# Short f32 side products counted as half a unit of fill in a recurrence, and one transposition a step later

## The chip, the cores and the metric

The kernel runs on one core of one Trainium2 chip. The metric is the device time of one execution in microseconds (us), lower is better. The kernel before takes 1494.18 us in the median of three runs (1492.56 to 1495.71).

## The reference

The input x has four batches of 256 rows of 512. Four layers are added to it one after the other, each on a layer norm of x: a cross-attention, a gated feed-forward with int4 weights (1792 wide), a recurrent attention decoder over the 256 rows, and a feed-forward with 16 experts of which two are taken for each row. The decoder is the part that matters here, since each of its 256 steps needs the one before:

```python
def step(carry, tgt):
    s, c, alpha = carry
    f = lax.conv_general_dilated(alpha, conv_w, (1,), 'SAME', dimension_numbers=('NCH', 'OIH', 'NCH'))
    e = jnp.einsum('a,bta->bt', va, jnp.tanh(enc_proj + (s @ Wa_s.T)[:, None, :] + jnp.einsum('bft,af->bta', f, Wa_f) + ba))
    e = jnp.where(mask, e, jnp.float32(-1e+30))
    alpha_new = jax.nn.softmax(e, axis=1)[:, None, :]
    g = jnp.einsum('bt,btd->bd', alpha_new[:, 0], hbatch)
    y = jnp.tanh(g @ L_gy_w.T + L_gy_b + s @ L_sy.T) @ L_yy_w.T + L_yy_b
    rec = tgt @ L_ys.T + s @ L_ss.T + g @ L_gs_w.T + L_gs_b
    ig, fg, cg, og = jnp.split(rec, 4, axis=1)
    c_next = _sig(fg) * c + _sig(ig) * jnp.tanh(cg)
    s_next = _sig(og) * jnp.tanh(c_next)
    return ((s_next, c_next, alpha_new), y)
```

The targets tgt are rows of the layer norm of x after the second layer. Row l of the fourth layer needs y of step l.

## The kernel before, in words

A front part computes the attention of all rows and the first feed-forward of the first quarter of the rows. Then the recurrence runs its 256 steps (`for l in range(S)`, once in each engine's program). An end part does the experts of the last quarter.

One step of the recurrence is a chain over three engines. TensorE adds the state's part (L1876, L1882), ScalarE takes a tanh twice, in f16 and in f32 (L1438, L1439), TensorE makes the scores (L1890, L1896, and L1899 once VectorE's low part of the tanh is ready), ScalarE takes the exponentials (L1443, L1444), TensorE multiplies with them (L1908, L1913) and with VectorE's low part el (L1917 and on), VectorE normalises, ScalarE and VectorE make the gates and the new state, and TensorE's L1933 carries the attention into the next step.

TensorE would wait at five places of a step. There it calls `fill(units, order, rest)`, at L1886, L1897, L1901, L1930 and L1934, called fill 1 to 5 below, for 1, 1, 2, 2 and 1.5 units: 7.5 units a step, counted in half units (`HALF_UNIT, UNIT = 1, 2`). A fill adds its units to `credit` and takes work from generators until the credit is used up; what each piece of work yields is what it costs. If nothing is due, it issues a product without use, `keep_busy` (L1854), of 512 columns for a unit (384 in fill 1).

The work comes from two generators. `main_work` has the two feed-forwards for the other quarters: f16 products of 256 columns for half a unit (L1647, L1685, the experts' weights L1701) and of 512 for a unit (L1664). `side_work` has short f32 products that get layer norms, the decoder's inputs and outputs and the experts' routing through TensorE:

- `turn`: transpositions of 128x128 blocks of a layer norm (L1723), four for each half of a quarter's rows;
- `gates_input`: after a turn, the f32 products for the gates (L1560, not changed), two for a unit;
- `prelude`: outputs of the decoder (L1760, L1762), then rows products (L1805, 65x128, each two instructions on TensorE), then a turn;
- `expert_routing`: router products (L1769, 16 columns, each two instructions), two for a unit, then two transpositions of the expert weights (L1777).

Fills 1 and 2 ask main work first, fills 3 to 5 side work first. Each generator is held back by `paced(step)`: it gives nothing before the step that a table sets (`LN2`, `GATES`, `Y`, `PRELUDE`, `first_step`). A main tile of 24 products is spread over two steps, 12 half units a step. In a step with two transpositions of a unit each, side and main work want 4 + 12 = 16 half units of 15, and main work falls behind its table by a product or two. The order in which TensorE issues is fixed by this when the program is built; the waits on semaphores stay in it, so an instruction whose wait is late holds all that stand behind it.

In `gates_input` the last turn (q = 3, p = 1, table entry 165, so step 172) also waits for `rin_ready`, which ScalarE raises after its second gate piece of the half before (L1360).

Of the kernel before, what the change touches and what calls it, by code (L numbers as in the profile page):

```python
# [81 lines left out]
def build(nc, a, out):  # L82
    with ExitStack() as ctx:
# [280 lines left out]
        def pace(q):  # L364

            return 4 if q == 2 else 2

        def prelude_step(q, name, p=None):

            if q == 3:  # L370
                return S
            n = PRELUDE[q][name]
            return Y[q] + (n if p is None else n[p])
# [10 lines left out]
        def gates_bank(q, p):  # L384
            return bank[5 if q == 3 else 5 + p]
# [13 lines left out]
        def ln3(q, p):  # L399
            return (12, 16, 22, 26)[q] + p  # L400

        def ln4(q, p):
            return (20, 24, 28, 30)[q] + p
# [14 lines left out]
        def paced(step):  # L418

            while now[0] < step:  # L420
                yield False
# [1060 lines left out]
        def _(pe):  # L1482
# [73 lines left out]
            def gates(slot, bk, signal):  # L1556

                for gp in range(2):
                    for kt in range(KT):
                        last = mm(bk[:, gp * P:(gp + 1) * P], lys[:, kt, gp * P:(gp + 1) * P], xT_rec[:, kt, :], start=(kt == 0), stop=(kt == KT - 1))  # L1560
                        if signal and gp == 1 and kt == KT - 1:
                            last.then_inc(s["rec_done"], 1)
                        yield True
# [68 lines left out]
            HALF_UNIT, UNIT = 1, 2  # L1632
# [83 lines left out]
            def turn(n, bk, t, per_step):  # L1716

                for kt in range(KT):
                    yield from paced(t + kt // per_step)
                    if kt == 0:  # L1720
                        pe.wait_ge(s["ln_ready"], n + 1)
                        pe.wait_ge(s["xT_ready"], n - 1)
                    last = nc.tensor.transpose(bk[:, kt * P:(kt + 1) * P], xn[:, n % 2, kt * P:(kt + 1) * P], ident[:])  # L1723
                    if kt == KT - 1:
                        last.then_inc(s["tr_done"], 1)
                    yield UNIT

            def next_input(q):
                for p in range(2):
# [5 lines left out]
            def gates_input(q):  # L1735
                for p in range(2):
                    t, slot, bk = GATES[q][p], 2 * q + p, gates_bank(q, p)
                    yield from paced(t + 7)
                    if q == 1:
                        pe.wait_ge(s["xl_ready"], 5 + p)  # L1740
                    elif q == 2:
                        pe.wait_ge(s["wT_low_ready"], 1)
                    else:
                        pe.wait_ge(s["xT_ready"], ln4(1, 1) + 1)
                    if q == 3 and p == 1:
                        pe.wait_ge(s["rin_ready"], slot)
                    yield from turn(ln3(q, p), bk, t + 7, 2)
                    work = gates(slot, bk, True)
                    for unit in range(8):
                        yield from paced(t + 11 + p + unit // 2)  # L1750
                        if unit == 0:
                            pe.wait_ge(s["xT_ready"], ln3(q, p) + 1)
                        next(work)
                        yield UNIT

            def outputs(q):

                bk, rows = y_bank(q), slice(q * QL, (q + 1) * QL)
                for h in range(2):
                    mm(bk[0:J, 0:QC], hy[:, h, :], ahist[:, rows, 4 * h:4 * h + 4], start=(h == 0), stop=False)  # L1760
                    yield UNIT
                mm(bk[0:J, 0:QC], lsyT[:], shist[:, rows, :], start=False, stop=True).then_inc(s["y_done"], 1)  # L1762
                yield UNIT
# [18 lines left out]
            def prelude(q):  # L1782
                work = outputs(q)
                for unit in range(3):
                    yield from paced(prelude_step(q, 'outputs') + 2 * unit // pace(q))
                    if unit == 0:
                        pe.wait_ge(s["hist_done"], (q + 1) * QL)
                        pe.wait_ge(s["kept"], (q + 1) * QL)
                        if q == 0:
                            pe.wait_ge(s["xl_ready"], 8)  # L1790
                        elif q == 1:
                            pe.wait_ge(s["rin_ready"], 6)
                        else:
                            pe.wait_ge(s["wT_low_ready"], 2)
                    next(work)
                    yield 2 * UNIT
                for p in range(2):
                    for part in range(4):
                        yield from paced(prelude_step(q, 'rows', p) + part // pace(q))
                        if part == 0:  # L1800
                            pe.wait_ge(s["u_ready"], q + 1)
                            pe.wait_ge(s["w1_in"], 32)
                            if q == 2 and p == 1:
                                pe.wait_ge(s["y_added"], 2 * q + 1)
                        last = mm(rows_bank(q, p)[:, P * part:P * part + P], uT[:, q % 2, p * P:(p + 1) * P], lyy[:, P * part:P * part + P],  # L1805
                                  start=True, stop=True)
                        if part == 3:
                            last.then_inc(s["yy_done"], 1)
                        yield UNIT
                for p in range(2):  # L1810
                    yield from paced(prelude_step(q, 'turn', p))
                    pe.wait_ge(s["y_added"], 2 * q + 2)
                    if q == 2:
                        pe.wait_ge(s["act_ready"], TILES + 2 * IT1)
                    yield from turn(ln4(q, p), turn_bank(q, p), prelude_step(q, 'turn', p), pace(q))

            def expert_routing(q):
                work = router(q)
                for unit in range(8):
                    yield from paced(prelude_step(q, 'router') + unit // 4)  # L1820
                    if unit == 0:
                        pe.wait_ge(s["xT_ready"], ln4(q, 1) + 1)
                        if q == 1:
                            pe.wait_ge(s["rin_ready"], 8)
                    next(work)
                    if unit % 2 == 1:
                        yield UNIT
                work = turn_weights(q)
                for unit in range(2):
                    yield from paced(prelude_step(q, 'turned'))  # L1830
                    if unit == 0:
                        pe.wait_ge(s["wsel_ready"], q + 1)
                    next(work)
                    yield UNIT

            def side_work():
                yield from next_input(2)
# [190 lines left out]
```

## Time and profile before

| | |
|---|---|
| median of 3 runs | 1494.18 us (1492.56 to 1495.71) |
| the profiled execution, its own time | 1494.22 us |
| its span | 1492.3 us |
| mean granted clock of TensorE | 0.936 |
| TensorE busy | 1372.9 us, 92% of the span |
| VectorE, ScalarE, GpSimd busy | 892.8, 585.8, 210.0 us |
| chain of waits that ended last: TensorE, VectorE, ScalarE | 83%, 7%, 5% |
| filler products (L1854) | 685, 194.7 us busy |

The recurrence runs from about 287 to 1440 us of the span. Busy times overlap between engines. Matmuls are pipelined: each lasts some 0.16 us longer than the time until the next can start, so in a row of several equal ones the time goes by their spacing. The granted clock is the share of full speed that the chip gave to TensorE in a stretch; 1.00 is 2.4 GHz and 0.50 is 1.2 GHz, and what lies between is a mean of the two.

### The profile page before, as it was taken

To read this page: it belongs to the slowest core of one execution; us is meant where nothing else is said; L and a number is where in the kernel's file an instruction comes from. 1 tells how busy PE (TensorE), PEld (TensorE's weight loads), DVE (VectorE), ACT (ScalarE), POOL (GpSimd) and SP (SyncE) were. 2 spreads that over 40 slices of the span, in tenths; PEclk is the share of its full clock that TensorE was granted. 3 is DMA by queue.
4 is the path that set the end of the run, shared out by engine and by line. 5 is a ranking of instruction groups with operands and counts; after the bars stand their busy time and mean duration, and the time that the engine had idled before them with its cause. 6 is when DMAs were issued, how large, how long until landed. Compare 5 with 4: busy or idle time off the path is not lost.

```text
span 1492.3 us, 41237 instructions
## 1 busy us (share of the span) xinstructions
PE 1372.9 (92%) x16128; PEld 864.9 (58%) x16128; DVE 892.8 (60%) x4447; ACT 585.8 (39%) x2367; POOL 210.0 (14%) x704
## 2 busy tenths in 40 slices
PE   3466887999999999999999999999999999999988
PEld 1345665566655666655566655556655665566546
DVE  3664754366655566575666657766655566566643
ACT  3553652234333344333334434443433333333321
POOL 1001002011111121111111112231110011111111
PEclk8666897999999999899999999999999999999999
DMA  8462220000000000000000001110000000000000
GB/s 280 190 219 77 78 77 4 1 2 2 2 2 2 2 2 2 2 2 2 2 2 2 2 19 51 55 36 2 2 16 2 2 2 9 9 2 2 9 9 15
DMA packets 23863, 44.77 MB, mean 30 GB/s; under 512 B 8788, under 2 KB 12035, under 8 KB 23668
## 3 DMA queue, kind: packets, MB, share of 16 engines
q1 hardware_dynamic: 23668, 42.14, 8.5%
q8 instruction: 126, 2.06, 0.6%
q14 instruction: 69, 0.57, 0.1%
HBM read 40.04 MB, written 2.10 MB: 28 GB/s over the span
## 4 chain that ended last, share of the span: by engine, by line
PE 83%; DVE 7%; ACT 5%; issue 4%; SPq 1%; DMA 1%; POOL 0%; DVEq 0%; ACTq 0%; POOLq 0%
PE bank L1933 10%; PE bank L1854 10%; PE bank L1647 9%; PE bank L1876 8%; PE bank L1664 6%; PE bank L1908 6%; PE bank L1685 4%; PE bank L1890 3%; PE bank L1624 3%; PE bank L1917 3%; PE bank L1896 2%; PE bank L1882 2%; PE bank L1630 2%; PE bank L1532 2%; ACT interT L1210 2%
## 5 line engine op out<-in xcount | busy, mean ns | idle before, releaser
L1854 PE MATMUL bank<-ctx_lgs,identh 128*128 128x512 f16 (+2 forms) x685 | 194.7, 358 | 0.0
L1933 PE MATMUL bank<-ker_mem,uh 128*128 128x128 f32 x1020 | 185.9, 306 | 1.0 <-DVE ker_mem L1133 0.8
L1933 PEld LDWEIGHTS bank<-ker_mem,uh 128*128 128x128 f32 x1020 | 138.3, 196 | 71.2 <-DVE ker_mem L1133 70.5
L1647 PE MATMUL bank<-xT,wbig 128*128 128x256 f16 x1008 | 168.9, 280 | 0.0
L1452 ACT ACTIVATE xs<-gat 64x8 f32<-64x8 f32 x255 | 52.9, 207 | 245.5 <-DVE gat L1129 245.4
L1438 ACT ACTIVATE ker_mem<-bank 128x128 f16<-128x128 f32 x256 | 71.0, 277 | 187.0 <-PE bank L1876 187.0
L1443 ACT ACTIVATE eh<-bank,nmx 128x8 f16<-128x8 f32 x256 | 68.4, 267 | 160.8 <-PE bank L1899 160.8
L1664 PE MATMUL bank<-wbig,interT 128*128 128x512 f16 x378 | 124.8, 393 | 0.0
L1133 DVE TENSOR_TENSOR ker_mem<-inv,ahn 128x128 f32<-128x128 f32 x510 | 124.0, 285 | 0.1
L709 POOL TENSOR_TENSOR sscale<-ex,rinv 128x8 f32<-128x8 f32 x256 | 51.1, 200 | 496.4 <-DVE rinv L1118 496.4
L705 POOL COPY sscale<-s 64x4 f32<-64x4 f32 x256 | 59.2, 231 | 388.4 <-DVE s L1148 388.4
L1908 PEld LDWEIGHTS bank<-eh,ctx_lgs 128*128 128x128 f16 x2048 | 69.5, 96 | 69.4 <-ACT eh L1443 68.9
L1115 DVE TENSOR_TENSOR el<-ex,eh 128x8 f16<-128x8 f32 x256 | 43.0, 168 | 105.9 <-ACT ex L1444 105.8
L1107 DVE TENSOR_TENSOR ker_mem<-enc,ker_mem 128x128 f16<-128x128 f32 x256 | 74.8, 292 | 45.2 <-ACT enc L1439 44.1
L1118 DVE RECIPROCAL rinv<-bank 128x4 f32<-128x4 f32 x256 | 46.7, 182 | 78.8 <-PE bank L1917 78.8
L1455 ACT ACTIVATE tc_sb<-xs 64x4 f32<-64x4 f32 x255 | 52.4, 205 | 105.6 <-DVE xs L1144 105.6
L1908 PE MATMUL bank<-eh,ctx_lgs 128*128 128x4 f16 x2048 | 90.2, 166 | 1.9
L1532 PE MATMUL bank<-vbd,interT 128*128 128x34 f32 x256 | 47.2, 343 | 45.2 <-ACT interT L1218 45.2
L1876 PEld LDWEIGHTS bank<-sh,was 64*128 64x128 f16 x512 | 28.4, 94 | 102.8 <-DVE sh L1147 97.1
L1104 DVE TENSOR_TENSOR rs<-bank,rin 128x8 f32<-128x8 f32 x256 | 42.1, 164 | 73.9 <-PE bank L1882 62.4
L591 POOL TENSOR_TENSOR interT<-work,interT 128x256 f16<-128x256 f32 x84 | 56.6, 674 | 187.4 <-ACT interT L1229 115.1
L1876 PE MATMUL bank<-sh,was 64*128 64x128 f16 x512 | 73.7, 225 | 8.4 <-DVE sh L1147 0.6
(232 smaller groups left out, 3130.3 us busy)
## 6 DMA issues: line engine op xcount, KB each, us to landing
kbd<-d_keys SPq DMA_DIRECT2D x32, 256.0 KB, 3.7
wbig<-d_gate_qT SPq DMA_DIRECT2D x4, 896.0 KB, 9.9
wbig<-d_up_qT SPq DMA_DIRECT2D x4, 896.0 KB, 20.6
wbig<-d_down_qT SPq DMA_DIRECT2D x1, 3584.0 KB, 13.1
sscale<-d_down_sT SPq DMA_DIRECT2D x4, 768.0 KB, 8.8
x_sb<-d_x SPq DMA_DIRECT2D x16, 128.0 KB, 2.9
d_out<-x_sb SPq DMA_DIRECT2D x16, 128.0 KB, 2.4
sscale<-d_gate_sT SPq DMA_DIRECT2D x2, 896.0 KB, 8.3
```

The lines of the kernel that those rows point to most:

```text
L1107: nc.vector.tensor_tensor(th_lo, th, th_hi, ALU.subtract).then_inc(s["th_lo_ready"], 1)
L1133: return nc.vector.tensor_tensor(qv[:, h, :, :], inv[:].unsqueeze(1).broadcast_to([P, B, TH]), ahn[:, 4 * h:4 * h + 4].unsqueeze(2).broadc ...
L1438: nc.scalar.activation(th_hi, bank[0][:, 0:P], ACT.Tanh).then_inc(s["th_s"], 1)
L1443: nc.scalar.activation(eh[:], bank[0][:, P:P + 8], ACT.Exp, bias=nmx[:, 0:1]).then_inc(s["eh_ready"], 1)
L1532: last = mm(bank[6 + pair // 8][:, (pair % 8) * 34:(pair % 8) * 34 + 34], pT[:, n % 2, j * P:(j + 1) * P], vbd[:, b, pair // 2, :], start= ...
L1647: last = mm(tile_bank(n)[:, lo:lo + QC], w[wi][:, kt, it * P:(it + 1) * P], x_part[q % 2][xi][:, kt, :], start=(kt == 0 and wi + xi == 0), ...
L1664: last = mm(bk[:], i_part[ii][:, it, p * P:(p + 1) * P], w[wi][:, it, :], start=(it == 0 and ii + wi == 0), stop=(it == tiles - 1 and ii = ...
L1685: last = mm(tile_bank(n)[:, lo:lo + QC], w[wi][:, kt, it * P:(it + 1) * P], x1_part[q][xi][:, kt, :], start=(kt == 0 and wi + xi == 0), st ...
L1854: mm(bank[7][:, 0:n], identh[:], hg2[:, 0].rearrange("p h g -> p (h g)")[:, 0:n], start=True, stop=True)
L1876: last = mm(bank[0][:, 0:P], was2[:, j, :], st[:].unsqueeze(2).broadcast_to([J, B, TH]), start=False, stop=(st is sl), skip_group_check=True)
L1908: mm(bank[2][:, 8 + 4 * gp:12 + 4 * gp], hg2[:, j, h, gp * P:(gp + 1) * P], e[:, 4 * h:4 * h + 4], start=False, stop=final, skip_group_che ...
L1933: mm(bank[0][:, 0:P], uh[:, h, :], qv[:, h, :, :], start=False, stop=False, skip_group_check=True)
```

## The change

Transpositions, rows products, pairs of router products and transpositions of expert weights yield `HALF_UNIT` instead of `UNIT`. The last turn of the gate inputs begins one step later, in step 173. The other costs, the tables and the sizes of the fills stay.

```diff
@@ turn
                     last = nc.tensor.transpose(bk[:, kt * P:(kt + 1) * P], xn[:, n % 2, kt * P:(kt + 1) * P], ident[:])
                     if kt == KT - 1:
                         last.then_inc(s["tr_done"], 1)
-                    yield UNIT
+                    yield HALF_UNIT
@@ gates_input
                     t, slot, bk = GATES[q][p], 2 * q + p, gates_bank(q, p)
-                    yield from paced(t + 7)
+                    yield from paced(t + 7 + (q == 3 and p == 1))
...
-                    yield from turn(ln3(q, p), bk, t + 7, 2)
+                    yield from turn(ln3(q, p), bk, t + 7 + (q == 3 and p == 1), 2)
@@ prelude
                         if part == 3:
                             last.then_inc(s["yy_done"], 1)
-                        yield UNIT
+                        yield HALF_UNIT
@@ expert_routing
                     next(work)
                     if unit % 2 == 1:
-                        yield UNIT
+                        yield HALF_UNIT
                 work = turn_weights(q)
...
                     next(work)
-                    yield UNIT
+                    yield HALF_UNIT
```

Only TensorE's order changes, in 74 of the 256 steps. Three places of it follow. L1647, L1685 and L1664 are main products, L1854 filler, L1890 to L1917 and L1933 the recurrence's own.

Step 9, fill 3, which follows L1899, with two transpositions; before:

```order
L1899 MATMUL bank<-vae,ker_mem 128x8
L1723 MATMUL bank<-ident,xn 128x128 x2
L1908 MATMUL bank<-eh,ctx_lgs 128x4 x8
L1913 MATMUL bank<-eh,onesb 128x4 x2
L1917 MATMUL bank<-el,onesb 128x4 x2
```

and with the change:

```order
L1899 MATMUL bank<-vae,ker_mem 128x8
L1723 MATMUL bank<-ident,xn 128x128 x2
L1647 MATMUL bank<-xT,wbig 128x256 x2
L1908 MATMUL bank<-eh,ctx_lgs 128x4 x8
L1913 MATMUL bank<-eh,onesb 128x4 x2
L1917 MATMUL bank<-el,onesb 128x4 x2
```

Two main products of 256 columns stand beside the transpositions; fill 5 of the step ends with a filler of 256 columns in place of the third main product. In steps with rows products it is the same with L1805.

Step 183, fills 1 to 3, with router products; before:

```order
L1769 MATMUL bank<-gwT,kbd 128x16 x2
L1890 MATMUL bank<-ker_mem,vah 32x32 x8
L1896 MATMUL bank<-vae,ker_mem 128x8 x2
L1769 MATMUL bank<-gwT,kbd 128x16 x2
L1899 MATMUL bank<-vae,ker_mem 128x8
L1854 MATMUL bank<-ctx_lgs,identh 128x512 x2
L1908 MATMUL bank<-eh,ctx_lgs 128x4 x8
```

and with the change:

```order
L1769 MATMUL bank<-gwT,kbd 128x16 x4
L1890 MATMUL bank<-ker_mem,vah 32x32 x8
L1896 MATMUL bank<-vae,ker_mem 128x8 x2
L1854 MATMUL bank<-ctx_lgs,identh 128x512
L1899 MATMUL bank<-vae,ker_mem 128x8
L1854 MATMUL bank<-ctx_lgs,identh 128x512 x2
L1908 MATMUL bank<-eh,ctx_lgs 128x4 x8
```

All four router products of the step stand in fill 1, and fill 2 has a filler of 512 columns.

Step 172, from its fill 2 on, where the moved turn began; before:

```order
L1685 MATMUL bank<-interT,wbig 128x256 x2
L1899 MATMUL bank<-vae,ker_mem 128x8
L1723 MATMUL bank<-ident,xn 128x128 x2
L1908 MATMUL bank<-eh,ctx_lgs 128x4 x8
L1913 MATMUL bank<-eh,onesb 128x4 x2
L1917 MATMUL bank<-el,onesb 128x4 x2
```

and with the change the turn begins in fill 1 of step 173:

```order
L1701 MATMUL bank<-interT,wbig 128x256
L1723 MATMUL bank<-ident,xn 128x128
L1890 MATMUL bank<-ker_mem,vah 32x32 x8
L1896 MATMUL bank<-vae,ker_mem 128x8 x2
L1723 MATMUL bank<-ident,xn 128x128
L1854 MATMUL bank<-ctx_lgs,identh 128x256
L1899 MATMUL bank<-vae,ker_mem 128x8
```

Its last two transpositions stand in fill 3 of step 174, beside a main product of 512 columns.

## Rows read from the trace of the kernel before

**Rows 1.** Stretches: bounds, us, busy by engine (instructions), granted clock, DMA; plain steps
```profile
382.84:471.51 88.67, 88.07 (x1158) 51.96 (x1155) 53.23 (x316) 33.01 (x152) 11.63 (x46) 1.00 0.01 2
690.13:694.57 4.44, 4.30 (x58) 2.31 (x55) 3.06 (x17) 1.98 (x8) 1.05 (x3) 1.00 0.00 0
```

**Rows 2.** Timeline of TensorE in step 5, a plain one: start, us, instruction
```profile
311.13 0.38 PE L1647 MATMUL bank<-xT,wbig 128*128 128x256 f16 x2
311.39 0.18 PE L1899 MATMUL bank<-vae,ker_mem 128*128 128x8 f16 x1
311.42 0.60 PE L1647 MATMUL bank<-xT,wbig 128*128 128x256 f16 x4
311.93 0.35 PE L1908 MATMUL bank<-eh,ctx_lgs 128*128 128x4 f16 x8
...
312.29 0.20 PE L1917 MATMUL bank<-el,onesb 128*128 128x4 f16 x2
```

**Rows 3.** Stretches with f32 side products, or just behind them
```profile
337.31:347.12 9.81, 9.66 (x124) 6.52 (x120) 5.90 (x33) 4.04 (x18) 1.43 (x5) 0.83 0.01 2
610.38:636.81 26.43, 26.32 (x309) 18.49 (x306) 15.05 (x83) 8.61 (x39) 3.90 (x13) 0.74 0.01 2
667.99:685.71 17.72, 17.23 (x222) 9.83 (x219) 9.66 (x61) 6.93 (x30) 1.51 (x8) 1.00 0.01 2
884.18:901.91 17.73, 17.47 (x230) 11.13 (x226) 11.08 (x64) 7.17 (x30) 2.32 (x8) 1.00 0.06 15
699.27:709.29 10.02, 10.00 (x119) 6.21 (x116) 5.19 (x32) 3.10 (x15) 1.42 (x5) 0.83 0.01 2
811.79:821.90 10.11, 9.79 (x126) 6.48 (x123) 5.58 (x32) 4.61 (x19) 1.43 (x5) 0.83 0.01 2
1062.78:1074.09 11.31, 10.28 (x120) 6.73 (x116) 5.96 (x34) 4.03 (x17) 1.42 (x5) 0.70 0.01 2
1119.06:1124.85 5.79, 5.79 (x65) 3.96 (x61) 2.50 (x15) 1.49 (x7) 0.38 (x2) 0.72 0.01 3
1282.06:1293.07 11.01, 11.01 (x120) 7.07 (x116) 5.30 (x33) 3.10 (x16) 2.10 (x6) 0.69 0.11 25
```

**Rows 4.** Stretches: router steps 90 and 183, at full clock
```profile
694.57:699.27 4.70, 4.70 (x65) 3.11 (x62) 2.42 (x16) 1.49 (x7) 1.05 (x3) 1.00 0.01 3
1114.22:1119.06 4.84, 4.81 (x65) 3.19 (x62) 2.51 (x16) 1.50 (x8) 0.38 (x2) 1.00 0.24 56
```

**Rows 5.** Timeline of TensorE in step 9, with two transpositions in fill 3
```profile
329.19 0.18 PE L1899 MATMUL bank<-vae,ker_mem 128*128 128x8 f16 x1
329.28 0.41 PE L1723 MATMUL bank<-ident,xn 128*128 128x128 f32 x2
329.73 0.35 PE L1908 MATMUL bank<-eh,ctx_lgs 128*128 128x4 f16 x8
```

**Rows 6.** Timeline of TensorE in step 90, router products in fill 3
```profile
695.40 0.18 PE L1899 MATMUL bank<-vae,ker_mem 128*128 128x8 f16 x1
...
696.33 0.34 PE L1908 MATMUL bank<-eh,ctx_lgs 128*128 128x4 f16 x8
...
696.58 0.19 PE L1917 MATMUL bank<-el,onesb 128*128 128x4 f16 x2
```

**Rows 7.** Timeline of TensorE in step 132, two rows products in fill 3
```profile
885.01 0.18 PE L1899 MATMUL bank<-vae,ker_mem 128*128 128x8 f16 x1
...
885.62 0.34 PE L1908 MATMUL bank<-eh,ctx_lgs 128*128 128x4 f16 x8
```

**Rows 8.** Timeline of step 172: TensorE and, first, ScalarE; idle before in brackets
```profile
1064.14 0.58 ACT L1360 ACTIVATE rin<-bank,gbias,gscale 128x128 f32<-128x128 f32 x1
...
1063.61 0.18 PE L1899 MATMUL bank<-vae,ker_mem 128*128 128x8 f16 x1
1064.82 0.41 PE L1723 MATMUL bank<-ident,xn 128*128 128x128 f32 x2 [1.03 <-ACT rin L1360]
...
1065.32 0.19 PE L1917 MATMUL bank<-el,onesb 128*128 128x4 f16 x2
```

## The prediction, before the change was run

> **What bounds the kernel now.** I read the page first, then the stretches of the recurrence, then single steps on TensorE. Steps are numbered 0 to 255, and step l begins where ScalarE starts its first tanh (L1438). The recurrence is most of the program, and nearly every step takes the same time: twenty plain steps take 88.67 us at a granted clock of 1.00, 4.43 us each [rows 1]. That length is the chain through TensorE, ScalarE and VectorE, not the amount streamed: the step at 690.13, step 89, whose five fills hold 14 half units instead of 15, takes 4.44 us too [rows 1]. So work in a fill is free as long as it ends before its wait does. How tight that is shows in a plain step: from the start of L1899 to the start of L1908, which waits for the exponentials, 0.54 us pass (311.39 to 311.93), with four 256-column products between; the sum products (L1917) start 0.36 us later, at 312.29, and wait for VectorE's el [rows 2].
>
> The second thing the page shows is a clock that is not always granted in full. I cut the recurrence into stretches at step starts: those much longer than 4.43 us per step are the ones with a granted clock under 1.00 [rows 3]: the engine ran part of them at 1.2 GHz instead of 2.4. Every one that I found but that of step 0 lies in steps that hold short f32 side products (transpositions, rows, router) or just after them. TensorE did not idle there: in 610.38 to 636.81 it was busy for 26.32 of 26.43 us, and still the clock was 0.74. What it did before the clock fell was f32 side work in the place of wide f16 products. The Trainium skill, "TensorE: Matmul & The Clock Gate", section "Part 4: PE-mode transpose", says that a transposition does not count as busy in the same way as a product; the trace agrees for the transposition steps 11 and 63, but the clock also fell in steps with rows and router products, which are no transpositions.
>
> **Low clock, priced.** From each stretch I take 4.434 us per step [rows 3]. Steps 11 and 12: 9.81 - 8.87 = 0.94; steps 63 and 64 are a second pair with the same length and clock, 0.94. Steps 72 to 76 (rows products): 26.43 - 22.17 = 4.26. Steps 116 and 117: 10.11 - 8.87 = 1.24. Steps 172 and 173: 11.31 - 8.87 = 2.44, of which 0.8 is a stall (below), so 1.64. These are the steps of transpositions and rows: 9.0 us. The router's: steps 91 and 92, 10.02 - 8.87 = 1.15; step 184, 5.79 - 4.43 = 1.36; steps 220 and 221, 11.01 - 8.87 = 2.14. The router products themselves cost 0.27 in one step and 0.41 in each of two at full clock (steps 90 and 183 [rows 4]), which leaves 0.88 + 0.95 + 1.73 = 3.6 us for the clock.
>
> **The change, part by part.** It alters what TensorE issues in 74 steps; the order on the other engines stays. No product is added to the computation: 64 transpositions, 24 rows products, 12 pairs of router products and 6 transpositions of weights count one half unit less, 106 in all, and the fills make that up with 33 filler products (L1854) of 512 columns, 39 of 256 and one of 192, since the main products get done sooner.
>
> *Transpositions.* In 24 steps a fill that held two transpositions or more now gets something beside them or more of them. Before, two transpositions take 0.41 us and L1908 starts 0.54 us after L1899, as in a plain step, although TensorE is done much earlier [rows 5]. Four 256-column products take 0.60, two of them 0.38 [rows 2], so two more cost 0.22; 0.41 + 0.22 = 0.63, against the 0.60 that the plain step hides. L1917 has 0.36 us after L1908 in the plain step and needs 0.25 (step 90 [rows 6]), so 0.11 of cover is left. Cost: nothing. If that cover is gone, some 0.1 us in each of 24 steps, 2.4 us.
>
> *Rows products (L1805).* Two of them (four instructions) bring L1908 to 0.61 us after L1899 [rows 7]; this is 0.07 late and hidden by the 0.11. With 512 columns more it is 0.61 + 0.22 + 0.25 = 1.08 us to L1917 instead of 0.90: 0.18 in each of seven steps (72, 73, 75, 132 to 135), 1.26. In steps 200 and 206 four of them now share fill 3. Eight router instructions fill the 0.93 us from L1899 to L1908 in step 90, 0.116 each [rows 6], and four more rows instructions are taken at that: 0.61 + 4 x 0.116 + 0.25 - 0.90 = 0.4 a step, 0.8 for both. Step 74 has its two rows products in fill 1, about 0.14.
>
> *Router products (L1769).* In steps 90 and 91 they already overfill fill 3: L1917 comes 0.25 + 0.93 = 1.18 us after L1899, 0.28 over plain, and the step is 4.70 [rows 6, 4]. Nothing hides a further 0.22: 0.43 for both. In steps 183, 184, 219 and 220 the second half of them moves from fill 2 to fill 1 and 512 columns of filler take their place: 0.22 each, 0.86.
>
> Overfull steps together: 1.26 + 0.8 + 0.14 + 0.43 + 0.86 = 3.5 us. The trace has no step with just these mixes; the bounds are nothing beyond what now stands (0, if the waits have slack that I don't see) and 3.5 + 2.4 = 5.9. I take 3.5, since the router rows show such a delay arriving in the step length almost whole.
>
> *The transposition a step later.* In step 172 the four transpositions of the last gate input begin with a wait for ScalarE's L1360, the second gate piece: it starts at 1064.14, runs 0.58, and L1723 starts at 1064.82 after 1.03 us of idle [rows 8]. L1908, L1917 and so the whole step queue behind it: L1917 comes 1.71 us after L1899 (1063.61 to 1065.32) against 0.90 in a plain step, 0.8 us. They now begin in step 173, long after L1360. ScalarE takes the result in the late half of step 174, and the last transposition is issued in fill 3 of 174, before it; on VectorE nothing moves. So 0.8 goes and no new wait comes.
>
> *The clock.* In a transposition or rows step the fill now streams 512 columns beside the f32 work, 0.22 us more of wide f16 products, which brings it back to what plain steps have, less at most the f32 work's own share. No plain step fell. My forecast is that the 9.0 us go and the router's 3.6 stay, since there the streamed share stays low for a whole step.
>
> **Sum.** 1494.22 (the profiled execution, span 1492.3; the median of the runs is 1494.18, so nothing has to be moved) - 9.0 - 0.8 + 3.5 = 1487.9 us. Its own range is 1486 to 1490.
>
> **Rivals.**
> *Router stretches go too.* The 512 columns in steps 90, 183, 219 and their like may be enough. Then 3.6 more go: 1484.3. Against it: two router steps in a row still hold sixteen f32 instructions with 16 columns each. Chance 0.08.
>
> *Some falls only move.* Steps 84 to 87 hold transpositions and kept the clock at 1.00, so did the rows steps 132 to 135 (17.73 us for four, 4.43 each), whereas steps 11 and 72 to 76 didn't [rows 3]: it is partly chance which group falls. If the longer, overfull steps 72 to 75, 132 to 135, 200 and 206 fall in their place, half of the 9.0 comes back: 1487.9 + 4.5 = 1492.4. Chance 0.2.
>
> *Slower: the filling does not hold the clock.* If it falls for some other reason than a lack of wide f16 products, the 12.6 us of low clock stay and only the price is new: 1494.2 - 0.8 + 3.5 = 1496.9. It decides from the point where the clock saves under 2.7 us, in the steps 72 to 76. For it speaks that TensorE was busy all the time where the clock fell. The Trainium skill, "TensorE: Matmul & The Clock Gate", section "HAM oscillation", puts a falling clock down to idle gaps between groups of products; by that rule more filling would change nothing here, and the result would be this one. The rows don't bear it out: step 172 has the longest gap and the clock fell there, but in 72 to 76 there is none [rows 3, 8]. Chance 0.1.
>
> *The change doesn't do what it says.* The same number of columns could pile up on TensorE as the bound: 33 x 512 + 39 x 256 + 192 = 27072 columns at 0.22 us per 512 are 11.6 us. The step at 690.13 excludes it for most: fewer columns there bought nothing [rows 1]. Chance 0.02, at 1505.
>
> **Chances.** The forecast has 0.6. A measurement of this kernel can tell about 0.2%, 3 us, from no change; faster by more means under 1491.2. Forecast and the first rival are there nearly whole, the second with a third of its chance: 0.75. Within 0.2%: the rest of the second and a little of the first, 0.16. Slower: 0.09 with the last two rivals and a price above 3.5. The range takes in the forecast and most of the second rival and leaves out the router's gain and the slower cases: 1485.2 to 1492.8.
>
> **What would show it.** Right: clock 1.00 in steps 9 to 12, 62 to 65, 72 to 76 and 116; a mean granted clock well over 0.936 in the recurrence; L1723 with no idle before it in step 173 and step 172 at 4.43; steps 132 to 135 at 4.6, 200 and 206 at 4.8, 90 at 4.9 and 183 at 5.05. Wrong: transposition steps over 4.5 at full clock, which says that 0.11 of cover isn't there; or stretches at half clock in the same number as before, elsewhere.

## The result, and the profile after

The changed kernel takes 1483.77 us in the median of five runs (1482.95 to 1484.96) against 1494.18 for the kernel before (1491.19 to 1495.71): a ratio of 0.9928, interval 0.9901 to 0.9955. The forecast was 1487.9 with a range of 1485.2 to 1492.8. The sign is right; the time lies 1.4 us under the range. Its profiled execution took 1483.51 us with a span of 1481.6, against 1494.22 and 1492.3; the mean granted clock rose from 0.936 to 0.947.

Stretches of the changed kernel, cut at step starts as in [rows 1, 3, 4] (bounds, us, busy by engine, granted clock, DMA). First the recurrence, whole, then twenty plain steps, 9 to 12, 72 alone, 72 to 76, 90, 91 and 92, 116 and 117, 132 to 135, 172, 173 and 174, 183, 184, 200, and 220 with 221:

```profile
283.45:1429.42 1145.97, 1135.82 (x14934) 697.17 (x14930) 722.64 (x4160) 449.77 (x1983) 173.46 (x618) 0.99 0.03 8
378.15:466.79 88.64, 88.00 (x1158) 51.93 (x1154) 53.24 (x316) 33.00 (x151) 11.62 (x46) 1.00 0.01 2
324.62:342.43 17.81, 17.67 (x252) 12.07 (x249) 12.01 (x67) 7.61 (x34) 2.86 (x10) 1.00 0.01 2
604.73:609.35 4.62, 4.59 (x68) 3.33 (x65) 2.46 (x16) 1.77 (x9) 1.05 (x3) 1.00 0.01 4
604.73:627.70 22.97, 22.83 (x315) 15.54 (x312) 14.76 (x83) 8.61 (x40) 3.89 (x13) 1.00 0.01 3
685.45:690.37 4.92, 4.90 (x66) 3.21 (x62) 2.41 (x16) 1.49 (x7) 1.04 (x3) 1.00 0.00 0
690.37:699.72 9.35, 9.29 (x121) 5.61 (x118) 5.10 (x32) 3.10 (x15) 1.42 (x5) 1.00 0.01 2
802.23:811.09 8.86, 8.80 (x128) 5.92 (x124) 5.49 (x32) 4.61 (x19) 1.43 (x5) 1.00 0.01 2
873.36:891.72 18.36, 18.28 (x236) 11.45 (x233) 11.05 (x64) 7.16 (x30) 2.30 (x8) 1.00 0.05 14
1052.53:1056.96 4.43, 4.40 (x65) 2.84 (x61) 3.08 (x18) 1.96 (x9) 1.05 (x3) 1.00 0.02 6
1056.96:1066.98 10.02, 10.00 (x117) 5.91 (x113) 6.01 (x34) 3.82 (x18) 1.43 (x5) 0.83 0.01 2
1102.69:1107.74 5.05, 5.02 (x66) 3.27 (x62) 2.51 (x16) 1.49 (x7) 0.38 (x2) 1.00 0.23 54
1107.74:1113.54 5.80, 5.80 (x66) 3.92 (x63) 2.50 (x15) 1.49 (x7) 0.38 (x2) 0.78 0.01 3
1180.74:1185.58 4.84, 4.82 (x70) 3.59 (x67) 3.09 (x18) 1.49 (x8) 1.05 (x3) 1.00 0.00 0
1271.92:1282.35 10.43, 10.40 (x121) 6.50 (x117) 5.24 (x33) 3.10 (x15) 2.10 (x6) 0.84 0.11 27
```

Each row gives the bounds, the length, the busy time of TensorE, its weight loads, VectorE, ScalarE and GpSimd with their instructions, the granted clock and the DMA share and rate. A plain step is as long as before. The clock is now 1.00 in steps 11, 12, 72 to 76, 91, 92, 116 and 117, where it was low in [rows 3]. It still falls in 173, 184 and 220, as it did before. The overfull steps show their price at full clock: 4.62 in step 72, 4.92 in step 90, 5.05 in step 183, 4.84 in step 200. Step 172 is plain again.

Why step 72 is 0.18 us longer and step 9 isn't stands in TensorE's timeline. Step 9 of the changed kernel:

```profile
325.45 0.18 PE L1899 MATMUL bank<-vae,ker_mem 128*128 128x8 f16 x1
325.55 0.41 PE L1723 MATMUL bank<-ident,xn 128*128 128x128 f32 x2
325.79 0.38 PE L1647 MATMUL bank<-xT,wbig 128*128 128x256 f16 x2
326.01 0.34 PE L1908 MATMUL bank<-eh,ctx_lgs 128*128 128x4 f16 x8
326.43 0.20 PE L1917 MATMUL bank<-el,onesb 128*128 128x4 f16 x2
```

L1908 starts 0.56 us after L1899 and L1917 0.98 us after it. In the kernel before L1917 was as late in this step (329.19 to 330.17), so the two products more are hidden. Step 72 of the changed kernel:

```profile
605.56 0.18 PE L1899 MATMUL bank<-vae,ker_mem 128*128 128x8 f16 x1
605.66 0.68 PE L1805 MATMUL bank<-interT,sscale 65*128 65x128 f32 x4
606.18 0.38 PE L1647 MATMUL bank<-xT,wbig 128*128 128x256 f16 x2
606.40 0.34 PE L1908 MATMUL bank<-eh,ctx_lgs 128*128 128x4 f16 x8
```

L1908 starts 0.84 us after L1899 instead of 0.61 [rows 7], which is 0.3 late against the plain step's 0.54. In step 200, with eight rows instructions in the fill, it is 1.06 (1181.57 to 1182.63):

```profile
1181.57 0.18 PE L1899 MATMUL bank<-vae,ker_mem 128*128 128x8 f16 x1
1181.67 1.13 PE L1805 MATMUL bank<-interT,sscale 65*128 65x128 f32 x8
1182.63 0.34 PE L1908 MATMUL bank<-eh,ctx_lgs 128*128 128x4 f16 x8
```

**Where the 10.7 us between the two spans went.** The recurrence is 1145.97 us long against 1153.00 (from 287.18 to 1440.18 before): 7.0 less. The end part is 52.2 us in both. The other 3.7 lie ahead of the first step, where no instruction differs. The next rows are everything ahead of the first tanh of step 0, the dense part of it, and the recurrence, of the kernel before:

```profile
0.00:287.18 287.18, 190.88 (x991) 137.14 (x991) 152.00 (x232) 126.75 (x360) 27.14 (x70) 0.77 0.35 120
206.80:244.40 37.60, 32.58 (x190) 26.90 (x191) 13.62 (x25) 15.81 (x50) 3.36 (x5) 0.73 0.04 8
287.18:1440.18 1153.00, 1139.62 (x14861) 699.39 (x14858) 723.07 (x4160) 449.85 (x1983) 173.63 (x618) 0.98 0.03 8
```

and of the changed kernel:

```profile
0.00:283.45 283.45, 190.34 (x991) 137.24 (x991) 151.93 (x232) 126.89 (x360) 27.16 (x70) 0.77 0.36 122
206.80:244.40 37.60, 31.30 (x207) 26.06 (x207) 16.50 (x32) 16.41 (x52) 4.10 (x6) 0.82 0.04 7
```

The mean clock of the front part is the same, but in the dense stretch from 206.80 to 244.40 it is 0.82 instead of 0.73, and TensorE gets through 207 products there instead of 190. Whether this is chance or belongs to the changed kernel is what the second and third profiles below are for.

### The profile page after: what moved, and what is told of

Its sections match the earlier page's. It is cut to its first block, busy times and chain, and to the rows that moved or that the text cites. A ratio compares the mean times of both kernels' runs of the same rounds, so it can differ in the third digit from the quotient of the medians.

```text
span 1481.6 us, 41383 instructions
## 1 busy us (share of the span) xinstructions
PE 1368.7 (92%) x16201; PEld 862.8 (58%) x16201; DVE 892.4 (60%) x4447; ACT 585.8 (40%) x2367; POOL 209.8 (14%) x704
## 4 chain that ended last, share of the span: by engine, by line
PE 84%; DVE 6%; ACT 4%; issue 3%; SPq 1%; DMA 1%; POOL 0%; DVEq 0%; ACTq 0%; POOLq 0%
PE bank L1854 10%; PE bank L1933 10%; PE bank L1647 9%; PE bank L1876 8%; PE bank L1664 7%; PE bank L1908 6%; PE bank L1685 4%; PE bank L1890 3%; PE bank L1624 3%; PE bank L1917 3%; PE bank L1896 2%; PE bank L1882 2%; PE bank L1630 2%; PE bank L1532 2%; ACT interT L1210 2%
## 5 line engine op out<-in xcount | busy, mean ns | idle before, releaser
L1854 PE MATMUL bank<-ctx_lgs,identh 128*128 128x512 f16 (+2 forms) x758 | 211.2, 352 | 0.0
L1933 PE MATMUL bank<-ker_mem,uh 128*128 128x128 f32 x1020 | 182.8, 302 | 0.6 <-DVE ker_mem L1133 0.6
L1933 PEld LDWEIGHTS bank<-ker_mem,uh 128*128 128x128 f32 x1020 | 134.7, 192 | 71.2 <-DVE ker_mem L1133 71.0
L1647 PE MATMUL bank<-xT,wbig 128*128 128x256 f16 x1008 | 165.3, 274 | 0.0
L1664 PE MATMUL bank<-wbig,interT 128*128 128x512 f16 x378 | 125.6, 391 | 0.0
L1908 PEld LDWEIGHTS bank<-eh,ctx_lgs 128*128 128x128 f16 x2048 | 69.4, 96 | 67.1 <-ACT eh L1443 64.4
L1908 PE MATMUL bank<-eh,ctx_lgs 128*128 128x4 f16 x2048 | 90.0, 166 | 0.3
L1876 PEld LDWEIGHTS bank<-sh,was 64*128 64x128 f16 x512 | 28.3, 94 | 101.8 <-DVE sh L1147 99.3
L1147 DVE SCALAR_TENSOR_TENSOR sh<-xs,tc_sb 64x4 f16<-64x4 f32 x255 | 39.3, 154 | 69.3 <-ACT tc_sb L1455 69.3
```

The source lines that it names most:

```text
L1647: last = mm(tile_bank(n)[:, lo:lo + QC], w[wi][:, kt, it * P:(it + 1) * P], x_part[q % 2][xi][:, kt, :], start=(kt == 0 and wi + xi == 0), ...
L1664: last = mm(bk[:], i_part[ii][:, it, p * P:(p + 1) * P], w[wi][:, it, :], start=(it == 0 and ii + wi == 0), stop=(it == tiles - 1 and ii = ...
L1854: mm(bank[7][:, 0:n], identh[:], hg2[:, 0].rearrange("p h g -> p (h g)")[:, 0:n], start=True, stop=True)
L1876: last = mm(bank[0][:, 0:P], was2[:, j, :], st[:].unsqueeze(2).broadcast_to([J, B, TH]), start=False, stop=(st is sl), skip_group_check=True)
L1908: mm(bank[2][:, 8 + 4 * gp:12 + 4 * gp], hg2[:, j, h, gp * P:(gp + 1) * P], e[:, 4 * h:4 * h + 4], start=False, stop=final, skip_group_che ...
L1933: mm(bank[0][:, 0:P], uh[:, h, :], qv[:, h, :, :], start=False, stop=False, skip_group_check=True)
```

## The experiments

All are edits of the kernel before or of the changed kernel, in four groups, each on another chip; the kernels of a group ran beside the kernel before in the same rounds, so times are compared within a group. In the expectations a "stretch of low clock" is the shortest fall that was seen, and a longer fall counts as several. To compare, I give the recurrence's length and the clock of its critical steps in each profile. Counted over the recurrence, the profiles have these stretches of low clock:

| kernel | stretches | recurrence, us |
|---|---|---|
| before: first profile, e1, e13 | 14, 32, 24 | 1153.0, 1170.1, 1163.5 |
| the move alone: e2 | 19 | 1156.8 |
| 16 columns beside: e9, e16 | 12, 15 | 1153.4, 1157.5 |
| 256 columns beside: e4, e15 | 7, 9 | 1150.0, 1153.5 |
| halved costs alone: e3, e14 | 10, 7 | 1152.9, 1149.7 |
| changed: first profile, e5, e12 | 4, 4, 8 | 1146.0, 1146.2, 1150.3 |
| transpositions alone: e7; fuller: e8 | 7; 7 | 1146.3; 1146.6 |
| changed, fuller: e6, e11; rows at a unit: e10 | 5, 2; 4 | 1147.8, 1144.3; 1144.5 |

Within a group fewer stretches go with a shorter recurrence: e13, e16, e15 and e14 have 24, 15, 9 and 7 stretches, and 1163.5, 1157.5, 1153.5 and 1149.7 us.

### Both kernels again: e1, e13 (before) and e5, e12 (changed)

No edit.

> The kernel before, unchanged, as a second profile. Theory A (the 3.7 us that the changed kernel gained ahead of its first step are chance: the clock fell at other moments of the front part): the front part, from the first instruction to the first tanh of step 0, takes between 283 and 288 us and differs from the 287.2 of the first profile by more than 0.5 us. Theory B (something fixed in the changed kernel shortens the front): the front takes 287.2 us again, within 0.5. Both: ratio to before 1.000 within 0.002.

> The kernel before a third time. Theory (it has more falls of the clock in most executions than the 14 stretches of its first profile): 14 to 35 stretches of low clock in the recurrence, recurrence 1153 us or more, front part another value between 281 and 289. Rival (32 stretches were an outlier): 10 to 16 stretches.

> The changed kernel as it is, beside kernel before in the same rounds. My theory (the change is worth what its steps show, 7 to 12 us in the recurrence, and the front part adds chance of some 2 us either way): ratio 0.990 to 0.995, the overfull steps 72, 132, 183 and 200 at 4.6, 4.6, 5.06 and 4.83 us again, at most 8 stretches of low clock in the recurrence and a front part that differs from the 283.4 us of its first profile. Rival (something fixed shortens the front by 3.7 us): front at 283.4 again within 0.5.

> The changed kernel a third time. Theory: the recurrence again about 1146 us with four to five stretches of low clock; the front part again another value between 281 and 289 us, which shows that it is chance. Rival: front part at 283.4 or 285.4 as a fixed property of a chip.

Measured against before in the same rounds: e1 1.0022 (0.9987 to 1.0056), e13 1.0021 (0.9994 to 1.0048), so a null comparison is null. The changed kernel: e5 0.9941 (0.9916 to 0.9965; 1489.13 against 1496.91), e12 0.9964 (0.9951 to 0.9977; 1492.4 against 1497.16). The gain is 4.8 to 10.4 us over three groups of runs.

The kernel before in its second and third profile, recurrence, steps 9 to 12 and steps 72 to 76; first e1:

```profile
287.62:1457.72 1170.10, 1157.59 (x14861) 713.35 (x14857) 723.52 (x4160) 449.98 (x1982) 173.43 (x618) 0.95 0.03 8
328.80:347.55 18.75, 18.40 (x244) 12.22 (x240) 12.08 (x67) 7.60 (x34) 2.85 (x10) 0.91 0.01 2
610.72:641.00 30.28, 30.28 (x309) 21.66 (x305) 15.15 (x83) 8.61 (x40) 3.90 (x13) 0.55 0.01 2
```

then e13:

```profile
286.01:1449.51 1163.50, 1149.20 (x14861) 706.78 (x14857) 723.49 (x4160) 451.59 (x1983) 174.55 (x618) 0.96 0.03 8
327.21:345.97 18.76, 18.40 (x244) 12.21 (x241) 12.08 (x67) 7.62 (x33) 2.87 (x10) 0.91 0.01 2
610.08:632.54 22.46, 22.26 (x309) 15.18 (x305) 14.70 (x83) 8.63 (x40) 3.93 (x13) 1.00 0.01 3
```

The same steps cost 30.28 us in one execution and 22.46 in another, with the clock alone between them. The recurrence of before took 1153.0, 1170.1 and 1163.5 us, so the profile that I read was a mild one; that of e1, on the other hand, is the longest of its twelve runs (1513.4 us, median 1503.1). The changed kernel's, here e5 and e12:

```profile
285.37:1431.56 1146.19, 1136.33 (x14934) 697.19 (x14930) 723.07 (x4160) 449.70 (x1982) 173.45 (x618) 0.99 0.03 8
```

```profile
288.29:1438.60 1150.31, 1140.55 (x14934) 700.48 (x14931) 723.34 (x4160) 450.47 (x1982) 173.44 (x618) 0.99 0.03 8
1064.10:1068.72 4.62, 4.59 (x61) 2.67 (x57) 2.84 (x17) 2.07 (x9) 0.38 (x2) 1.00 0.00 0
```

1146.0, 1146.2 and 1150.3 for the recurrence: lower and less scattered. e12 was expected to repeat the 1146 us with four or five stretches, and had eight. The front part took 283.4, 285.4 and 288.3 us in the changed kernel and 287.2, 287.6 and 286.0 in the kernel before; over all eighteen profiles it went from 281.7 to 288.4. Theory A of e1 asked for a difference of more than 0.5 us from the first profile and got 0.4, but e5, e12 and e13 settle it: the same instructions take several microseconds more or less, and nothing fixed in the changed kernel gives 3.7 us. It is no fixed property of a chip either: e9 to e12 ran on one, and their front parts took 283.3 to 288.4 us. The last row of e12 is step 173 at full clock: 4.62, so the moved turn costs 0.2 us there (in e2 0.13), with the experts' weight product L1701 and a transposition in fill 1.

### One part alone: e2 (the move), e3 and e14 (the costs)

```diff
-                    yield from paced(t + 7)
+                    yield from paced(t + 7 + (q == 3 and p == 1))
...
-                    yield from turn(ln3(q, p), bk, t + 7, 2)
+                    yield from turn(ln3(q, p), bk, t + 7 + (q == 3 and p == 1), 2)
```

is all of e2; e3 and e14 have the rest of the change and not this.

> Only the last turn of the gate inputs begins a step later; all costs as before. My theory: step 172 takes 4.43 us instead of 5.48, the 1.03 us of idle before its transposition is gone, and the fall of the clock in steps 172 and 173 goes with it or shrinks: 0.8 to 2.4 us less, 1492.0 to 1493.4. Rival: the wait returns in step 173 or 174, and nothing is gained, 1494.2. In either case steps 72 to 76 lose clock as before.

> Only the costs are halved; the last turn stays in step 172. My theory: the whole gain on the clock and the whole price of the overfull steps are here, so 0.8 us more than the changed kernel if the clock holds in steps 172 and 173 and up to 2.4 us more if it doesn't: 1484.6 to 1486.2. Rival (the move brought the surplus over the forecast): 1488 or more.

> Costs halved, turn in step 172, again. Theory: 5 to 10 stretches, 6 to 8 us faster than before in the same rounds.

e2: 0.9974 (0.9949 to 1.0), e3: 0.9949 (0.9927 to 0.997), e14: 0.9938 (0.9912 to 0.9963). Steps 172 and 173 of e2, then step 172 of e3:

```profile
1058.80:1063.22 4.42, 4.39 (x65) 2.83 (x62) 3.08 (x18) 1.96 (x8) 1.05 (x3) 1.00 0.01 2
1063.22:1067.78 4.56, 4.48 (x60) 2.59 (x57) 2.84 (x17) 2.07 (x10) 0.38 (x2) 1.00 0.01 4
```

```profile
1057.03:1063.38 6.35, 5.32 (x67) 3.94 (x63) 3.10 (x18) 1.96 (x8) 1.05 (x3) 0.73 0.01 4
```

The move removes the stall, as foreseen, and no new idle time comes with it. e2's ratio reaches up to 1.0, so its gain of 1.8 us is not clear of noise, and its profile has 19 stretches: the move isn't what holds the clock. With the costs halved and no move, step 172 keeps its idle and has the fall of the clock besides. The absolute times that I had expected were off, since the runs of these rounds were slower as a whole (before: 1498.64); by ratio e3 and e14 (0.9949 and 0.9938) have as much as e5 (0.9941). e14 is 9.2 us under before where 6 to 8 were expected. In e2 the clock fell in steps 11 to 13 and not in 72 to 76 (steps 9 to 12 and 72 to 76):

```profile
326.86:346.84 19.98, 19.74 (x244) 13.33 (x240) 12.10 (x67) 7.60 (x33) 2.85 (x10) 0.79 0.01 2
612.00:634.43 22.43, 22.25 (x309) 15.18 (x305) 14.68 (x83) 8.61 (x39) 3.90 (x13) 1.00 0.01 3
```

So it does not fall in a fixed group of steps.

### What in the filling holds the clock: e4, e15 (256 columns) and e9, e16 (16 columns)

Costs and order of the kernel before, and a filler behind each transposition, each rows product and each pair of router products, with 256 columns in e4 and e15 and 16 in e9 and e16. The edit at the transpositions, which the three other places repeat:

```diff
                     if kt == KT - 1:
                         last.then_inc(s["tr_done"], 1)
+                    keep_busy(256)
                     yield UNIT
```

> Side products cost a full unit as before and main products stand where they stood, but each of them is followed by a filler product of 256 columns (one for each pair of router products). No turn is moved. My theory (what counts is the wide f16 columns streamed beside the f32 work, whatever they compute): clock 1.00 in steps 9 to 12, 62 to 65 and 72 to 76 as in the kernel with halved costs alone, and the same time as that one within 1.5 us, about 1485. Rival (what counts is that main products stay on their table and fill the steps behind): the clock falls as before, and the price of the longer fills comes on top, 1496 to 1498.

> As the kernel with a filler product beside each side product at full cost (e4), but each of these fillers has 16 columns instead of 256. My theory (the clock is held by the columns streamed, not by the number of products): the clock falls as in the kernel before, 13 or more stretches of low clock in the recurrence, and the time is that of before within 3 us, some 1494 to 1498. Rival (any product beside the f32 ones breaks up what lets the clock fall): at most 8 stretches and about 1489, as with 256 columns.

> 256 columns of filler beside each side product, full cost, again. Theory (columns count): 5 to 10 stretches and 6 to 8 us faster than before, as with costs halved, and at least 2 us faster than with 16 columns.

> 16 columns of filler beside each side product, again. Theory (columns count): 10 or more stretches, one of them or more in steps 9 to 76, and at least 2 us slower than with 256 columns. Rival (a short f16 product beside the f32 ones is enough): no fall in steps 9 to 76 and the same time as with 256 columns within 1.5 us.

With 256 columns: 0.9943 (0.9916 to 0.997) and 0.9957 (0.9937 to 0.9978), as with halved costs within the intervals (e4 is 0.25 us behind e3 and e15 3.0 us behind e14, in the same rounds). Main products need not be brought forward for the gain; most or all of it comes from columns without use as well. With 16: 0.9956 (0.9938 to 0.9975) and 0.9973 (0.9953 to 0.9994). In the one group that holds both, e15 took 1494.95 and e16 1495.75, 0.8 apart and not the 2 that I had set as the mark. The profiles say more than the medians. Recurrence and steps 9 to 12 in e15:

```profile
285.76:1439.23 1153.47, 1140.45 (x14967) 703.84 (x14963) 722.39 (x4160) 451.65 (x1983) 174.56 (x618) 0.99 0.03 8
326.97:344.80 17.83, 17.67 (x252) 12.07 (x249) 12.02 (x67) 7.63 (x34) 2.88 (x10) 1.00 0.01 2
```

and in e16, with steps 72 to 76:

```profile
283.93:1441.42 1157.49, 1144.05 (x14967) 705.25 (x14964) 723.53 (x4160) 451.66 (x1982) 174.52 (x618) 0.98 0.03 8
327.00:345.76 18.76, 18.60 (x252) 12.67 (x248) 12.10 (x67) 7.62 (x34) 2.87 (x10) 0.91 0.01 2
608.15:631.83 23.68, 23.54 (x317) 16.42 (x314) 14.77 (x83) 8.65 (x39) 3.93 (x13) 0.93 0.01 3
```

The number of products is the same (x252 in both), and here the clock held in steps 9 to 12 with the wide ones and not with the narrow ones. In every profile with at least 256 columns per side product (the three of the changed kernel and e3, e4, e14, e15) steps 9 to 12 and 72 to 76 are at 1.00. But e9 was at 1.00 there too. By count the wide fillers left 7 and 9 stretches, the narrow ones 12 and 15, which is for the columns, in two profiles each. The medians don't show it: both narrow ratios lie clear under 1, so narrow fillers help too, and they pay less in overfull steps (step 72: 4.52 us in e9, 4.61 in e4). That the width of the products holds the clock, and not a product of any width in between, is likely and not shown.

### Which steps need it, and more room: e6, e11, e7, e8, e10

In e6 and e11 the changed kernel gets more filling in every step:

```diff
-                fill(UNIT, main_first, 384)
+                fill(UNIT, main_first)
...
-                fill(UNIT + HALF_UNIT, side_first)
+                fill(2 * UNIT, side_first)
```

In e7 rows and router products are back at `UNIT` (two lines of the change), in e8 that with the filling of e6, in e10 the rows products alone are back at `UNIT`, with the filling of e6.

> The change, and besides fill 5 gets 2 units instead of 1.5 and the filler of fill 1 has 512 columns instead of 384. My theory: at full clock a plain step stays at 4.43 us, since fill 5 ends 0.2 us before its wait, and the clock falls less often than in the changed kernel, so 0 to 3 us faster than that. Rival: the later fill 5 holds up the state's part (L1876) and each of 255 steps gets 0.02 to 0.1 us longer, 5 to 25 us slower.

> Only transpositions count half; rows and router products count a full unit as before; the turn is moved. My theory: the price of the overfull steps is gone (3.5 us), but the clock falls again in steps 72 to 76 and after router steps, 3 to 6 us: from equal to the changed kernel to 3 us slower. Steps 132 and 200 at 4.43, 90 at 4.70, 183 at 4.84 at full clock. Rival (rows steps would have kept the clock without the filling, the turns are all that counted): 3 us faster than the changed kernel and clock 1.00 in 72 to 76.

> As the one before, with fill 5 at 2 units and the filler of fill 1 at 512 columns in every step. My theory (columns beside the f32 work count wherever in the step they stand, and fill 5 has room for 256 more): rows steps keep the clock more often than without, at 4.43 us, so 1 to 4 us faster than the kernel with turns alone at half and up to 2 us faster than the changed kernel. Rival: only columns in the same fill count; then the clock falls in 72 to 76 as before and it equals the kernel with turns alone at half.

> The fuller kernel (e6) once more, in the same rounds as the changed kernel. My theory: 2 to 4 us faster than that, with a plain step of 4.43 us. Rival: the difference of 4 us seen between the two was chance of the clock, and they agree within 1.5 us.

> The fuller kernel (e6), but rows products count a full unit, so that steps 72, 73, 75, 132 to 135, 200 and 206 are not overfull. My theory: 1.3 + 0.8 us of price are gone, and the clock stays in these steps as it did in the kernel with turns alone at half: 1 to 2 us faster than the fuller kernel. Rival: the clock falls there again, for example at 198 to 202, and it is 0 to 3 us slower than the fuller kernel.

| | median, us | ratio to before | interval |
|---|---|---|---|
| e5, changed kernel | 1489.13 | 0.9941 | 0.9916 to 0.9965 |
| e6, fuller | 1485.03 | 0.9910 | 0.9877 to 0.9942 |
| e7, transpositions alone | 1487.98 | 0.9921 | 0.9888 to 0.9953 |
| e8, the same, fuller | 1488.21 | 0.9929 | 0.9904 to 0.9954 |
| second group: e12, changed kernel | 1492.4 | 0.9964 | 0.9951 to 0.9977 |
| e11, fuller | 1486.17 | 0.9925 | 0.9909 to 0.9941 |
| e10, fuller, rows at a unit | 1486.47 | 0.9928 | 0.9911 to 0.9944 |

The fuller kernel is 4.1 and 6.2 us under the changed one in the same rounds (0 to 3 and 2 to 4 expected), and the best of each group; in the second group the intervals don't overlap. Recurrence and steps 9 to 12 of e11:

```profile
283.28:1427.55 1144.27, 1142.23 (x14966) 698.93 (x14962) 723.44 (x4160) 449.70 (x1983) 173.45 (x618) 1.00 0.03 8
324.60:342.40 17.80, 17.78 (x252) 12.07 (x248) 11.99 (x67) 7.60 (x33) 2.86 (x10) 1.00 0.01 2
```

Fill 5 had the room: steps 9 to 12 take 17.80 us as in the changed kernel with TensorE busy for 17.78 instead of 17.67. The extra columns stand in every step, though, and fill 1 got 128 more: that it is fill 5 alone that helps isn't shown. In e7 rows and router steps are no fuller than before, and it is 1.15 us under the changed kernel, where 0 to 3 us above it was expected; the intervals overlap. So no gain of the rows and router part of the change is shown. Its steps 72 to 76:

```profile
608.82:631.28 22.46, 22.27 (x309) 15.17 (x305) 14.70 (x83) 8.62 (x39) 3.93 (x13) 1.00 0.01 3
```

22.46 against 22.97, and the clock held; but e13, the kernel before, had the same 22.46, so one execution doesn't show that it will. e10 has the lower price in these steps and no better median than e11: the 2 us that I had looked for are not there, or lie within the chance of the clock. e8 has no gain over e7, where 1 to 4 us were expected, and its clock fell in 90, 183, 184, 206 and 220, the router steps above all.

## Why the prediction was wrong, step by step

- **Low clock as the thing to gain: right.** In all three profiles of the changed kernel steps 9 to 12 and 72 to 76 are at 1.00, with 4, 4 and 8 stretches in the recurrence against 14, 32 and 24, and the filler of e4 and e15 does much the same without halved costs. The rival "slower: the filling does not hold the clock" is out. In the kernel before, TensorE was busy all the time ahead of the fall in step 72 and after it:

```profile
606.00:613.00 7.00, 6.97 (x109) 4.92 (x108) 4.08 (x25) 3.25 (x14) 1.25 (x4) 1.00 0.00 0
613.00:616.00 3.00, 3.00 (x22) 2.00 (x19) 1.65 (x9) 1.06 (x5) 0.18 (x1) 0.50 0.03 8
```

In e1 it was busy for 30.28 of 30.28 us in steps 72 to 76 at a clock of 0.55. The Trainium skill, "TensorE: Matmul & The Clock Gate", section "HAM oscillation", ties a falling clock to idle gaps. As a full account this doesn't agree with these rows.
- **What the lack of wide products does not explain.** I overlooked step 214. It holds no f32 side product and takes 5.09 us before and after, because TensorE waits 0.61 us for VectorE's el. In seven of the eighteen profiles (e3, e9, e10 and e12 to e15) the clock fell in it all the same; here the wait before, and the step in e12:

```profile
1256.79 0.20 PE L1917 MATMUL bank<-el,onesb 128*128 128x4 f16 x2 [0.61 <-DVE el L1115]
1250.43:1256.52 6.09, 5.48 (x59) 3.24 (x55) 3.07 (x17) 1.50 (x8) 1.16 (x4) 0.72 0.01 3
```

So the clock falls behind a short idle time as well, and the change does nothing about that. The prediction's "No plain step fell" holds for the profile that it was read from.
- **Price of the overfull steps: right.** Forecast 0.18 in each rows step of fill 3, measured 0.18 in step 72, 22.97 - 22.46 = 0.51 over steps 72 to 76 (against e13, at full clock) where 0.68 was forecast, and 18.36 - 17.73 = 0.63 over steps 132 to 135 where 0.72 was forecast; 0.4 in step 200, measured 0.41; 0.22 in steps 90 and 183, measured 0.22 and 0.21.
- **Transpositions at no cost: right.** 17.81 for steps 9 to 12, where step 9 was 4.51 long before too; L1908 came 0.56 us after L1899 in it, earlier than the 0.63 forecast; steps 116 and 117 take 8.86.
- **The stall of step 172: right**, 5.48 to 4.43; though part of the 5.48 was low clock (granted clock 0.88 in that step). I left out 0.2 us that the moved turn costs in step 173.
- **Router stretches stay: half right.** 91 and 92 were free of falls in the first profile (9.35, of which 0.5 is router work), and step 221 too (220 and 221: 10.43 against 11.01, although 0.22 of price came on top); 184 and 220 fell again. That is 0.9 + 0.8 = 1.7 of the 3.6 us gone.
- **The 9.0 us go: not all.** In 173 one stretch stayed: 10.02 for 173 and 174, less two plain steps and the 0.2 above, about 0.95.
- **The sum for the recurrence: nearly right, in part by luck.** Forecast -9.0 - 0.8 + 3.5 = -6.3, measured 1145.97 - 1153.00 = -7.0. By the last three points it would have been -9.0 + 0.95 - 1.7 - 0.8 + 0.2 + 3.3 = -7.05, with 3.3 for the price (0.51 + 0.63 above, 0.8 in steps 200 and 206, and an estimated 0.22 in each of six router steps): what went in the router steps and what stayed in 173 offset each other in part.
- **The step that failed** is the one that turned this sum into a time: "1494.22 (the profiled execution ...; the median of the runs is 1494.18, so nothing has to be moved) ... Its own range is 1486 to 1490." It held everything outside the changed steps at what one profile showed. The changed steps are not all that moves: the front part went by up to 6.7 us over the profiles, the end part between 52.2 and 54.0. In the profiles of the first comparison the front part gave 3.7 us of the 10.7; without it the profiled execution would have taken 1487.2, inside the range. In two other groups of rounds the same kernel ended at 1489.1 and 1492.4, above the forecast. What sets the level of a group stays open: the five runs of the first one lie within 2.0 us of each other and all under 1485, so it was more than one lucky execution, and only one of them has a profile. The falls of the kernel before are scattered too (1153.0 to 1170.1 in the recurrence), and one profile of it cannot size what a cure is worth. A range of 1482 to 1493, chosen now with hindsight, holds all three groups.

## What to carry to other kernels

Where a profile shows TensorE busy and its clock falling, look at what stands around the falls, and price a piece of work by that as well as by the time it holds the engine. Here most falls stood in or just behind steps with short f32 products, and wide products beside them brought the stretches of low clock in the recurrence from 14 to 32 down to 4 to 10. Put them in the gaps whose wait ends later, not in those that are already full: the transpositions' 512 columns more cost nothing, the rows' and the router's up to 0.4 us a step, without a gain that is shown. Look for the fill that ends before its wait before letting a full one run over. Here this is fill 5: in step 9 of the kernel before its last three products start at 331.83, are 0.11 us apart, and L1876 starts at 332.35, so some 0.2 us are left, an estimate; with 256 columns more there and 128 in fill 1 the time fell by 4.1 and 6.2 us. And where a profile shows falls of the clock, take several profiles of the unchanged kernel first, and widen the range by what unchanged parts do between them.

## What was not expected of the hardware

The same instructions in the same order took 281.7 to 288.4 us in the front part, and steps 72 to 76 of the kernel before took 26.43, 30.28 and 22.46 us, with nothing but the moments of the clock's falls between them. Once the clock is low in such steps it can stay low for five of them (0.55 over 30.28 us), although TensorE isn't idle for a moment. Why it stays low there in one execution and comes back after one stretch in another, no run shows.
